# A first pass that reads four arrays: half of the pair tiles move behind the image tiles, beside the statistics

## What is computed

```
mu, var over all of pair_rep = _gn(x);  x' = (pair_rep - mu) * rsqrt(var + EPS) * ln_w + ln_b     # layer 0
bias   = einsum('hc,bcij->bhij', wb, x')                       # layer 0, 4 heads: from x, ln_w and ln_b
scores = einsum('bhcij,bhcik->bhijk', q, k) * scale + bias[:, :, None, :, :]
bias   = einsum('nijz,zh->nhij', pair_repr, bias_proj)         # layer 1, 8 heads: from pair_repr alone
sim    = softmax(sim) + bias                                   # layer 1
```

## Time and profile before

| | us |
|---|---|
| median of 3 runs | 4940.08 (4938.53 to 4940.24) |
| the profiled execution | 4934.87 |
| its span | 4932.9 |
| first instruction of first_pass | 24.1 |
| first_pass ends, gs0 begins | 421.3 |
| layer0 issues its first load | 466.87 |

### The profile page before, as it was taken

How to read it: one execution, slowest core, us unless ns; L and a number is a source line. 1 busy time by engine, 2 the same in 40 slices (tenths; PEclk the granted TensorE clock), 3 DMA queues, 4 the chain that set the end, 5 groups by cost and what they waited for, 6 DMA issues and landing times. The chain is left out here.

```text
span 4932.9 us, 149816 instructions
## 1 busy us (share of the span) xinstructions
PE 4651.9 (94%) x44087; PEld 3925.1 (80%) x44087; DVE 4024.4 (82%) x12910; ACT 3523.2 (71%) x11216; POOL 3464.3 (70%) x5926
## 2 busy tenths in 40 slices
PE   4663999999999999999999989999999999999999
PEld 2332888888888888888888868888888888888887
DVE  4445888888888988888888868888888888888887
ACT  2222888888888888888888866666666666666665
POOL 3332888888888888888888846666666666666665
PEclk8776999999999999999999989999999999999999
DMA  8995111111111111111111101111111111111111
GB/s 330 356 355 173 53 51 60 56 54 60 51 60 52 59 56 55 60 51 60 51 59 52 59 29 53 51 51 51 47 49 51 51 51 51 51 51 51 51 50 40
DMA packets 237352, 382.70 MB, mean 78 GB/s; under 512 B 18756, under 2 KB 156616, under 8 KB 224968
## 3 DMA queue, kind: packets, MB, share of 16 engines
q1 hardware_dynamic: 237256, 381.63, 23.0%
HBM read 309.21 MB, written 72.35 MB: 77 GB/s over the span
## 5 line engine op out<-in xcount | busy, mean ns | idle before, releaser
L1337 POOL TENSOR_SCALAR l_probs<-l_probs,l_inv 128x256 f32<-128x256 f32 x2048 | 943.2, 478 | 735.7 <-DVE l_inv L1242 730.2
L1161 ACT ACTIVATE l_probs<-bank,l_neg_max 128x256 f32<-128x256 f32 x2048 | 947.0, 481 | 486.2 <-DVE l_neg_max L1236 486.2
L563 POOL TENSOR_SCALAR l_probs<-l_probs,l_inv 128x256 f32<-128x256 f32 x2048 | 947.5, 476 | 279.6 <-DVE l_inv L814 279.6
L732 ACT ACTIVATE l_probs<-l_probs,l_neg_max 128x256 f32<-128x256 f32 x2048 | 1020.8, 518 | 10.3 <-DVE l_neg_max L806 10.0
L806 DVE CUSTOM_DVE_ANT_0 l_probs<-bank,bias 128x256 f32<-128x256 f32 x2048 | 779.6, 418 | 202.8 <-PE bank L673 199.1
L1236 DVE TENSOR_REDUCE l_neg_max<-bank 128x2 f32<-128x512 f32 x1024 | 646.6, 684 | 92.3 <-PE bank L1070 92.3
L1249 DVE TENSOR_TENSOR l_probs_t<-bank,bias 128x512 f32<-128x512 f32 x1024 | 674.6, 682 | 35.4 <-PE bank L1080 5.4
L673 PE MATMUL bank<-ident,l_probs 128*128 128x128 f32 x4096 | 629.5, 276 | 8.4 <-DVE l_probs_t L828 7.3
L1080 PE MATMUL bank<-ident,l_probs 128*128 128x128 f32 x4096 | 531.7, 273 | 3.2 <-POOL l_probs L1337 1.6
L673 PEld LDWEIGHTS bank<-ident,l_probs 128*128 128x128 f32 x4096 | 463.7, 141 | 44.7 <-issue 8.4
L686 PE MATMUL bank<-l_probs_t,l_v 128*64 128x256 f32 x4096 | 498.5, 385 | 0.2 <-issue 0.2
(11 more groups left out here) (196 smaller groups left out, 14011.6 us busy)
## 6 DMA issues: line engine op xcount, KB each, us to landing
fp_x<-in_x_dram SPq DMA_DIRECT2D x32, 1024.0 KB, 6.9
fp_ln_w<-in_L_conv_ln_w_dram SPq DMA_DIRECT2D x32, 1024.0 KB, 8.9
fp_ln_b<-in_L_conv_ln_b_dram SPq DMA_DIRECT2D x32, 1024.0 KB, 10.8
fp_pair<-in_L_conv_pair_repr_dram SPq DMA_DIRECT2D x32, 1024.0 KB, 13.4
l_x<-in_x_dram SPq DMA_DIRECT2D x128, 256.0 KB, 2.9
l_ln_w<-in_L_conv_ln_w_dram SPq DMA_DIRECT2D x128, 256.0 KB, 3.4
l_ln_b<-in_L_conv_ln_b_dram SPq DMA_DIRECT2D x128, 256.0 KB, 3.5
x<-l_y SPq DMA_DIRECT2D x128, 256.0 KB, 2.0
```

The costliest lines, as they stand in the source:

```text
L563: last = nc.gpsimd.tensor_scalar(probs[:, h, c], probs[:, h, c], inv[:, h, c:c + 1], 1.0, ALU.mult, ALU.mult)
L732: last = nc.scalar.activation(probs[:, h, c], probs[:, h, c], ACT.Exp, bias=neg_max[:, h, c:c + 1], scale=-1.0, accum_out=total[:, h, c:c ...
L1161: last = nc.scalar.activation(probs[:, h, c], b_s[h % 4][:, c * W:(c + 1) * W], ACT.Exp, bias=neg_max[:, h, c:c + 1], accum_out=total[:, h ...
L1337: last = nc.gpsimd.tensor_scalar(probs[:, h, c], probs[:, h, c], inv[:, h, c:c + 1], 1.0, ALU.mult, ALU.mult)
```

## The change

- In first_pass the 32 image tiles now run with only 16 pair tiles, one behind every second image tile. The other 16 pair tiles come after the last image tile.
- Pair tiles have four buffers instead of two, so four are loaded ahead, and `load_pair(tile + 4)` is issued before `store_pair(tile)`, which waits for ACT. Image loads stand ahead of image stores as before. The pair bias has its own bank, output buffers and semaphores.
- All four copies of transposed pair data are on ACT. DVE has none.
- DVE aggregates every four image tiles (32 bn_aggr over 24 numbers) into `pieces`; the last aggregation is over 8 pieces.
- The block for gs0 is gone. Its operations stand in first_pass: DVE's come after the last image tile; PE's two matmuls behind pair tiles 18 and 19, ACT's two Sqrt behind 20 and 22. SP loads the image parts back in the turn of pair tile 17.
- The load of the pair bias (2 x 1 MB) moves from gs0 to gs1, where PE's transposes wait for it.
- The memset of the statistics (L156) moves from prepare_weights to the start of DVE's work in first_pass, with one more, of `pieces`.

```diff
-            load_pair(0, 0)
-            load_pair(1, 1)
-            def body(t, first, last):
-                for i in range(2):
-                    if not last:
-                        load(2 * t + i + 2, i)
-                    store(2 * t + i, i)
+            for i in range(PAIR_BUFS):
+                load_pair(i, i)
+            def body(t, first, last):
+                for k in range(2 * PAIR_BUFS):
+                    if not (last and k >= 2 * PAIR_BUFS - 2):
+                        load_image(2 * PAIR_BUFS * t + k + 2, k % 2)
+                    store_image(2 * PAIR_BUFS * t + k, k % 2)
+                    if k % 2:
+                        load_pair(PAIR_BUFS * (t + 1) + k // 2, k // 2)
+                        store_pair(PAIR_BUFS * t + k // 2, k // 2 % 2)
+            for tile in late_pairs:
+                if tile + PAIR_BUFS < TILES:
+                    load_pair(tile + PAIR_BUFS, tile % PAIR_BUFS)
+                if tile > late_pairs[0]:
+                    store_pair(tile - 1, (tile - 1) % 2)
+                if tile == late_pairs[1]:
+                    for i in range(2):
+                        sp.wait_ge(stored[i], 16 * STRIPS * TILES // 2)
+                    for part, to in ((W_PART, bias_w), (X_PART, m.bias0), (B_PART, bias_b)):
+                        for a in range(KC):
+                            sp.dma_start(to[:, a], image_parts[part, ...]).then_inc(parts_loaded, 16)
...
+            # PE
+            over_tiles(pe, image_tile, pair_tile)
+            pair_turns(late_pairs[0], late_pairs[0] // PAIR_BUFS, 0)
+            for tile in late_pairs:
+                if tile + 1 < TILES:
+                    pair_turns(tile + 1, (tile + 1) // PAIR_BUFS, (tile + 1) % PAIR_BUFS)
+                pair_project(tile, tile // PAIR_BUFS, tile % PAIR_BUFS)
...
+                for g in range(NG):
+                    last = nc.vector.bn_aggr(pieces[:, g, t, 1:3], stats[:, g, 0:PERIOD, :])
...
-        finish_statistics(nc, m, "gs0", lambda g: stats[:, g, 0:W // 8, :], True, (image_parts, pair_bias))
```

More of the change, by code:

```diff
@@ L228, in first_pass @@
 def first_pass(nc, m, image, pair, image_parts, pair_bias, stats):
     ROWS, TILES = TILE_ROWS, W // TILE_ROWS
[L237 to L239 removed]
+    STRIPS = ROWS // 2
+    PERIOD, PAIR_BUFS = 4, 4
+    X_PART, W_PART, B_PART = range(3)
+    b_part, b_pair, b_turned = m.psum[0:3], m.psum[3], m.psum[4:8]
     with ExitStack() as ctx:
         sem = lambda name: ctx.enter_context(nc.semaphore(f"fp_{name}"))
+        sems = lambda name: [sem(f"{name}{i}") for i in range(2)]
@@ L251, in first_pass @@
-        projected = [sem(f"projected_{part}") for part in ("x", "w", "b", "pair")]
-        bank = lambda j: m.psum[4 + j]
+        evac = sb("evac", [P, 3, 2 * W])
+        pair_evac = sb("pair_evac", [P, 2 * W])
+        pieces = ctx.enter_context(nc.sbuf_tensor("fp_pieces", [P, NG, TILES // PERIOD, 3], F32))
+        bias_w, bias_b = (of[0][:].rearrange("p (a h) k -> p a h k", a=KC) for of in (wt, bt))
+        pair_loaded = [sem(f"pair_loaded{i}") for i in range(PAIR_BUFS)]
+        stored, pair_stored = sems("stored"), sems("pair_stored")
@@ new lines, in _, with image_tile, finish_statistics @@
+        @block.gpsimd
+        def _(pool):
+            def image_tile(tile, t, i):
+                pool.wait_ge(measured, tile + 1)
+                nc.gpsimd.tensor_tensor(xt[i][:], xt[i][:], wt[i][:], ALU.mult).then_inc(weighted, 1)
+            over_tiles(pool, image_tile, lambda tile, t, i: None)
+def finish_statistics(nc, m, pieces, pair_bias):
+    with ExitStack() as ctx:
+        sem = lambda name: ctx.enter_context(nc.semaphore(f"gs1_{name}"))
+        statistics = Statistics(nc, ctx, m, "gs1")
+        pair_loaded, bias_mm, bias_out = sem("pair_loaded"), sem("bias_mm"), sem("bias_out")
+        b_bias = m.psum[2:8]
@@ L256, in _ @@
         def _(sp):
-            def load_pair(tile, i):
-                wait(sp, transposed, PAIRS * (tile - 1))
-                sp.dma_start(raw[i][:], pair[bass.ds(ROWS * tile, ROWS)].rearrange("q (p e) z -> p q e z", e=2)).then_inc(pair_loaded[i], 16)
-            def load(tile, i):
-                for part in (X_PART, W_PART, B_PART):
-                    wait(sp, projected[part], tile - 1)
-                image.load(sp, tile, i)
-                load_pair(tile, i)
-            def store(tile, i):
-                sp.wait_ge(evacuated, tile + 1)
-                for c in range(PAIRS):
-                    rows, mine = bass.ds(ROWS * tile + 2 * c, 2), evac[i][32 * c:32 * c + NH1]
-                    sp.dma_start(image_parts[:, :, rows, :].rearrange("s h r k -> h s (r k)"), mine[0:NH0, 0:3]).then_inc(stored[i], 16)
-                    sp.dma_start(pair_bias[:, rows, :].rearrange("h r k -> h (r k)"), mine[:, PAIR_PART]).then_inc(stored[i], 16)
@@ L287, in _ @@
+        @block.vector
+        def _(dve):
+            statistics.vector(dve, pieces, False)
+        @block.scalar
+        def _(act):
+            for h in range(NH1):
+                act.wait_ge(bias_mm, h + 1)
+                nc.scalar.activation(m.bias1[:, :, h], b_bias[h % 6][:].rearrange("p (a c) -> p a c", a=KC), ACT.Copy).then_inc(bias_out, 1)
+            statistics.scalar(act, 0)
         @block.tensor
         def _(pe):
-            def project(part, tile, weights, rows):
-                wait(pe, evacuated, tile)
-                for c in range(PAIRS):
-                    last = nc.tensor.matmul(m.psum[part][32 * c:32 * c + 32, :], weights, rows[:, 2 * c:2 * c + 2, :].rearrange("p r k -> p (r k)"),
-                                            start=True, stop=True, tile_position=(0, 32 * c))
-                last.then_inc(projected[part], 1)
@@ L473, in layer0 @@
+            pe.wait_ge(pair_loaded, 16 * KC)
+            for h in range(NH1):
+                wait(pe, bias_out, h - 5)
+                for kc in range(KC):
+                    for qc in range(KC):
+                        last = nc.tensor.transpose(b_bias[h % 6][:, kc * W + qc * P:kc * W + (qc + 1) * P], m.bias1[:, qc, h, kc * P:(kc + 1) * P], m.ident[:])
+                last.then_inc(bias_mm, 1)
+            statistics.tensor(pe, 0)
+            statistics.tensor(pe, 1)
 def layer0(nc, m, x, ln_w, ln_b, x1, stats):
```

361 lines of the change are left out of this document (194 added, 167 removed).

## The result

The changed kernel takes **4904.18 us** (median of 4 runs, 4901.4 to 4906.43), beside 4939.31 us for the kernel before on the same chip (4 runs, 4937.98 to 4940.24).

A forecast was written before the change was run, and what follows sets the result against it. The prediction took first_pass as a stream of loads followed by a 45.6 us statistics tail; -14.9 us there plus 8.3 in gs1 gave -6.6, so 4933.5 us from 4940.1, range 4914 to 4947.

The forecast's parts named there:

- The image stream: First_pass image tiles: a buffer's round trip of 22.5 us per two tiles outlasts 21.3 of transfers; tile 31 lands at 372.
- layer0: The block after first_pass: same instructions as before, so no change, with +-3 us allowed for layer0 and layer1.
- The offset: Profiled execution against median: the median of runs shown lies 5.2 us above the profiled 4934.87, giving 4940.1 as base.
- the late stage: Pair tiles left behind the last image tile: 80 us from tile 31's landing to layer0's first load, bounds 74 and 86.
- the idle DMA behind tile 31: After the last image tile lands: nothing queued behind pair tiles 16 to 18, so DMA idles about 12 us.
- the last bias operation: DVE's statistics work beside the late stage: ends about 20 us ahead of the block's end, so it costs nothing.
- gs1's size: Pair bias load of 2 MB in gs1: all on the path, 8.3 us added, bounds 7 and 11.
- PE's dry spell: Late stage: image parts go ahead of pair tile 22, so PE runs dry for 5 us; 2 us added.
- B: Image stream: queue stays full and transfers rule at 21.3 us per two tiles; 4916.5 us, chance 0.24.
- C: Late stage: PE stays at its lower clock, 5.6 us per pair tile instead of 3.3; 4964 us, chance 0.06.
- D: Image stream: stores hold SP so it becomes late, 1 to 2 us per double tile; 4947 to 4961, chance 0.11.
- E: End of first_pass: late roots leave DVE building the bias when the stream ends, up to 10 us; 4944, chance 0.05.

The follow-up runs named there:

- e4: Changed kernel with the product of x and ln_w made by DVE instead of POOL, right behind the statistics; 4907.69 us.
- e1: The changed kernel itself run again, on the chip of the three experiments beside it; 4908.17 us.
- e2: Kernel before with 59 already met waits in DVE's program, putting layer0's DVE code at the changed kernel's place modulo 256; 4927.41 us.
- e3: Changed kernel with 197 already met waits in DVE's first_pass, putting layer0's DVE code at the place modulo 256 of the kernel before; 4922.71 us.
- e8: Changed kernel with the product on DVE and 224 already met waits, putting layer0's DVE code back at 18 modulo 256; 4897.09 us.
- e13 to e18: Changed kernel with DVE's code shifted by 16, 64, 128, 96, 112 met waits, then 96 again in rounds; 4903.46, 4919.98, 4906.35, 5020.77, 4910.57, 5027.67 us.
- e7: Changed kernel with the 2 MB pair bias load issued in layer0, behind the loads of its first tiles, instead of in gs1; 4896.01 us.
- e6: Changed kernel with 24 instead of 16 pair tiles beside the image tiles and 8 left behind them; 4893.7 us.
- e11: Changed kernel with 24 pair tiles beside, seven pair buffers, pair bias loaded in layer0, product on DVE and 224 met waits; 4886.39 us.
- e9: Changed kernel with each odd image tile's pair tile before the projection of x, its reload and stores still behind the image reload; 4905.92 us.

## Why the prediction was wrong

The miss is 29.3 us (4933.5 against 4904.2). It divides as follows.

**The image stream, 9.6 us with the start (a term mis-sized).** "The round trip is 22.5 us per two image tiles; the larger limit rules": the mechanism holds (e4, DMA share 0.91), the size does not. It is 21.8 in the profiled execution, 21.7 in e1, over 14 rounds 9.3 us, and tile 3 landed 0.3 sooner. Both halves were over-long by some 0.2 to 0.4: I took every odd projection as cold (two of the eleven from tile 9 to 29 took 1.06), rounded the statistics and the product up and SP's wake-up to 0.3 (0.2 measured), and I took reload to landing from the start of the program. The bounds 21.3 to 22.8 did hold it, so this miss alone would have stayed in the range.

**layer0, 9.5 us (a step that failed).** "layer0 and layer1 have the same instructions; I allow them +-3." The same instructions at another address. The stalls of before were in its trace, four times 3 us "issue" on DVE, and I had not looked at a stretch that the diff leaves alone. e2, e3 and e8 show the cause, e13 to e18 its size: a shift by 96 instructions cost 119 us (5027.67 against 4908.17). With the stream's miss this gives 4914.4, at the lower end of the range.

**The offset, 7.5 us (luck of the executions).** I took the profiled execution of before to lie 5.2 us under the median; that of after lies 2.2 above its own. It took the time out of the range. The rest, 2.6 us, is layer1 (1.6), the late stage (0.5) and gs1 (0.4); the parts come to the 29.3 but for rounding.

**Right:** the landings of tiles 2 and 3 (48.2 and 56.7 against 48 and 57); the idle DMA behind tile 31 and the reload of pair 19 (375.53: +13.2, forecast +14.5); the last bias operation at 423.3, 18.5 us ahead of the end; gs1's size (+7.9 against +8.3, and e7 takes all of it back).

**Right in part by luck:** the late stage (79.5 against 80). Its sum slips by 0.9 us (15.5 + 52 is 67.5, not 68.4; the last pair tile landed at +68.0), and PE's dry spell is 9.1 us, not 5: the load of pair tile 22 landed at 401.2, behind the parts as forecast, but ACT's wait for a store behind the same parts, which the prediction does not have, ended at 401.6. In gs1 the load took 9.0 us from issue to landing, not 8.3 (the 2.3 us in the forecast stand in no row), and the transposes behind it 5.76 us instead of 6.65, which made up for it.

**The rivals.** B (transfers rule) did not come: 21.7, not 21.3, though its time is nearer to the result. C did not: behind the dry spell late tiles took 2.9 to 3.5 us, one 4.1, the turning 1.97, at a granted clock of 0.96. D was right that stores hold SP, 3.97 to 5.89 us for the four of a pair tile, and wrong that it was late: from tile 8 on it issued a reload 0.6 us late at most. E did not stick out; it did as soon as e6 shortened the stage. The price that the Trainium skill, "DMA: Bandwidth & Descriptors", section "Anatomy of one DMA", gives would have made the bias load 6.8 us (an estimate); that section gives it for DMAs issued by GpSimd, and these are issued by SP. The trace has 9.0 us, and gs1 +7.9, so the row of streams of 1 KB pieces was the better guide.

## What to carry to other kernels

Before an edit is sized, look for stalls named "issue" behind the ends of loops in the whole trace, and for packets of the instruction queue inside loops, also where the diff does nothing: an edit that adds instructions to an engine moves all its later code, and a gain or loss of 10 us, once 119, can be that alone. A kernel that seems to gain nothing (e4) is to be read by stretches and run again with its code put back by met waits.

Where a round trip and the transfers lie within 3% of each other, shortening one pays only down to the other; then move bytes out of the idle times instead (24 pair tiles beside, 11 us; the bias load into a quiet stretch, 8 us). And a load of several MB issued in one go makes every store behind it late: ask who waits for those stores, and what hangs on it once the stage is shorter.

## What the runs showed of the hardware

- DVE stands still for up to 3.4 us, with nothing to wait for, at the first point behind a left loop that lies at 67 to 73 modulo 128 instructions of its built program, and 2.5 us per iteration in one placement of a loop of 264 that begins at that point. An 8 KB packet of the instruction queue starts 1.7 to 1.9 us before each of the stalls in layer0 ends. The Trainium skill, "Runtime: NRT & Kernel Launch", section "Instruction fetch mechanics", says that code is fetched ahead in blocks of 256 instructions and that a taken branch out of the window forces a fetch stall. A stall behind a loop, and a fetch with it, agree; the period here is 128 (shifts by 0 and 128 give 2416.1 and 2415.5 us and the same place); with blocks of 256 the shift by 128 would have moved the stall.
- A store issued behind 3 MB of loads in SP's queue landed so late that its buffer came free 8.8 to 9.6 us after it was wanted (e11 8.75, changed kernel 9.56); SP itself was held 3.97 to 5.89 us in issuing the four stores of a pair tile behind an image load.
- The 16 DMA engines moved 352 GB/s at a share of 1.09 with pair tiles and image parts, in 1 KB pieces, and 405 at 1.02 in e9 while the last image tiles (8 KB pieces) came in:

```profile
350.00:360.00 10.00, 3.17 (x24) 0.46 (x16) 5.55 (x45) 1.19 (x2) 4.49 (x1) 0.83 1.02 405
```
